# First cross attention, query stage: the key products of half 1 move behind half 0's token products of the next pair of heads

## The reference, cut to what matters

```python
q_hk = (hidden_q @ Wq.T).reshape(b, s, H, K)
q_big = jnp.einsum('bshk,hkq->bshq', q_hk, w_kc_q)
kv_rope = kv_c * cos[None] + _rotate_half(kv_c) * sin[None]
q_r = jnp.einsum('bshq,hqr->bhsr', q_big, W_qr)
k_r = jnp.einsum('bld,hdr->bhlr', kv_rope, W_kr)
scores = jnp.einsum('bhsr,bhlr->bhsl', q_r, k_r)
```

## Time and profile before

| | |
|---|---|
| median of 3 runs | 1651.32 us (1651.06 to 1651.63) |
| span of the profiled execution | 1651.2 us, 24551 instructions |
| TensorE busy | 1590.1 us, 96% |
| VectorE, ScalarE, GpSimd busy | 942.8, 731.2, 665.9 us |
| the query stage | from 354.8 to 434.5 us of the span |
| TensorE's granted clock there | 1.00 |

### The profile page before, as it was taken

The page is one execution under the profiler, slowest core; times in us unless marked ns, Lnnn a source line. Parts: engine busy times, 40 slices in busy tenths (PEclk is TensorE's granted clock), DMA queues, the critical chain, the costliest instruction groups (busy, mean ns, idle before and its releaser), DMA issues.

```text
span 1651.2 us, 24551 instructions
## 1 busy us (share of the span) xinstructions
PE 1590.1 (96%) x9832; PEld 1353.0 (82%) x9832; DVE 942.8 (57%) x1535; ACT 731.2 (44%) x1227; POOL 665.9 (40%) x483
## 2 busy tenths in 40 slices
PE   7999999989999999989999989998989999999998
PEld 7898666878899998768889976887668888888887
DVE  6555664366545455677768566354766455554554
ACT  3113655322587765666511156332635334353342
POOL 3875542441498873421137633212512422222321
PEclk9999999999999999999999999999999999999999
DMA  4110003123222007200001100110001111111111
GB/s 166 52 65 28 2 2 116 56 84 127 95 89 65 14 1 267 93 1 1 1 13 65 51 27 1 50 39 32 21 23 43 45 64 46 51 46 51 51 58 45
DMA packets 28580, 88.52 MB, mean 54 GB/s; under 512 B 4154, under 2 KB 4282, under 8 KB 28215
## 3 DMA queue, kind: packets, MB, share of 16 engines
q1 hardware_dynamic: 28468, 86.96, 15.4%
HBM read 85.11 MB, written 1.84 MB: 53 GB/s over the span
## 4 chain that ended last, share of the span: by engine, by line
PE 83%; DVE 8%; ACT 5%; issue 3%; POOL 1%; ACTq 0%; DVEq 0%; POOLq 0%
PE PS L261 19%; PE PS L263 18%; PE PS L262 18%; PE PS L266 7%; PE PS L1125 4%; PE PS L1462 3%; PE PS L1477 2%; PE PS L561 2%; PE PS L952 1%; PE PS L585 1%; PE PS L1709 1%; PE PS L1697 1%; PE PS L551 1%; DVE sm L1731 1%; PE PS L569 1%
## 5 line engine op out<-in xcount | busy, mean ns | idle before, releaser
L307 POOL TENSOR_TENSOR HL<-stg,HL 128x1024 fp32r<-128x1024 f32 (+2 forms) x111 | 243.8, 2199 | 543.5 <-ACT HL L302 525.5
L261 PE MATMUL PS<-XT,HL 128*128 128x448 f32 x608 | 225.0, 370 | 4.3 <-DVE XT L342 3.7
L263 PE MATMUL PS<-XT,HL 128*128 128x448 f32 x608 | 223.1, 367 | 0.0
L262 PE MATMUL PS<-XT,HL 128*128 128x448 f32 x608 | 223.1, 367 | 0.0
L302 ACT ACTIVATE HL<-stg 128x1024 fp32r<-128x1024 f32 (+2 forms) x111 | 104.5, 944 | 216.6 <-PE PS L263 200.9
L261 PE MATMUL PS<-HL,XT 128*128 128x512 f32 (+1 forms) x380 | 137.8, 363 | 2.2 <-DVE XT L1981 1.4
L263 PE MATMUL PS<-HL,XT 128*128 128x512 f32 (+1 forms) x380 | 134.8, 355 | 0.0
L262 PE MATMUL PS<-HL,XT 128*128 128x512 f32 (+1 forms) x380 | 134.8, 355 | 0.0
L261 PEld LDWEIGHTS PS<-XT,HL 128*128 128x128 f32 x608 | 115.0, 189 | 16.6 <-DVE XT L342 4.9
L262 PEld LDWEIGHTS PS<-XT,HL 128*128 128x128 f32 x608 | 115.1, 189 | 9.2
L263 PEld LDWEIGHTS PS<-XT,HL 128*128 128x128 f32 x608 | 114.9, 189 | 9.2
(11 more groups left out here) (299 smaller groups left out, 3813.7 us busy)
## 6 DMA issues: line engine op xcount, KB each, us to landing
stg<-in_wst SPq DMA_DIRECT2D x87, 512.0 KB, 3.2
stg<-in_wst SPq DMA_DIRECT2D x16, 352.0 KB, 3.0
stg<-in_wst SPq DMA_DIRECT2D x16, 320.0 KB, 3.2
wsum<-in_wfc SPq DMA_DIRECT2D x8, 512.0 KB, 3.7
wsum<-in_wpj SPq DMA_DIRECT2D x8, 512.0 KB, 3.5
raw<-in_wfc SPq DMA_DIRECT2D x8, 512.0 KB, 7.5
stg<-in_wst SPq DMA_DIRECT2D x16, 256.0 KB, 2.6
raw<-in_wpj SPq DMA_DIRECT2D x7, 512.0 KB, 7.0
```

Of the source, the lines that this page charges most:

```text
L261: e.matmul(out, lh, rh, start=start, stop=False)
L262: e.matmul(out, lh, rl, start=False, stop=False)
L263: return e.matmul(out, ll, rh, start=False, stop=stop)
L307: e.tensor_tensor(slot(k)[:, 1, 0:n], stg[k % NSTG][:, 0:n], slot(k)[:, 0, 0:n].bitcast(F), A.subtract).then_inc(*done("pool_w", k))
```

## The change

The key products of half 1 of pair hp are issued in the next pair, behind the token products of its half 0; those of half 0 stay behind the token products of half 1. The side products are split: token_query(hp+1) goes beside half 0, key_query(hp+2) beside half 1, both ahead of the last two token products of a half. ScalarE's and VectorE's orders follow. stream_plan and sync, with the order of the loads, stay as they are, and so do all instructions in number and size.

```diff
--- before.py
+++ after.py
@@ -923,106 +923,107 @@
             e.tensor_tensor(Krh[hp % 3][:, 1, :], stg[k % NSTG][:, 576:704], Krh[hp % 3][:, 0, :].bitcast(F),
                             A.subtract).then_inc(*done("dve_q", "K", hp))
 
+        def key_product(e, hp, half):
+            e.wait_ge(*upon("dve_q", "qr", hp, half))
+            if half == 0:
+                e.wait_ge(*upon("dve_q", "K", hp))
+            if hp:
+                e.wait_ge(*upon("dve_q", "o", hp - 1, half))
+                e.wait_ge(*upon("act_q", "o", hp - 1, half))
+            kr, qr = Krh[hp % 3], qrh[half]
+            for j, (a, c) in enumerate(((0, 0), (0, 1), (1, 0))):
+                for e_ in range(2):
+                    r0 = slice(64 * e_, 64 * e_ + 64)
+                    last = e.matmul(PS[:, kbank(half, e_, hp), 0:HT], kr[r0, a, :], qr[r0, c, :], start=j == 0, stop=j == 2)
+                    if j == 2:
+                        last.then_inc(*done("pe_q", "k", hp, half, e_))
+
         def pe_q(e):
-            def beside(st):
-                if st < 8:
-                    yield from key_query(e, st)
-                if st <= 8:
-                    yield from token_query(e, st - 1)
-
-            for st in range(2, 10):
-                side = beside(st)
-                hp, i = st - 2, st % 2
-                n_side = 6 * (st < 8) + 8 * (st <= 8)
-                n = n_done = 0
-                e.wait_ge(*upon("dve_q", "M", hp))
-                for half in range(2):
-                    if hp:
-                        e.wait_ge(*upon("dve_q", "qr", hp - 1, half))
-                    elif half:
-                        ln_turn(e, "lnx", NT - 1, xn[0], NT - 1)
-                        e.wait_ge(*upon("dve_ln", "lnx", NT - 1, "lo"))
-                    else:
-                        e.wait_ge(*upon("dve_ln", "lnx", 3, "lo"))
-                    for kc in range(4):
-                        hs = slice(half * HT, (half + 1) * HT)
-                        out = PS[:, 3 + half, 0:HT]
-                        terms = ((0, 0), (0, 1), (1, 0))
-                        for j, (a, c) in enumerate(terms):
-                            last = e.matmul(out, Mhl[i][:, a, kc, :], XT[:, c, kc, hs], start=kc == 0 and j == 0,
-                                            stop=kc == 3 and j == 2)
-                            if kc == 3 and j == 2:
-                                last.then_inc(*done("pe_q", "q", hp, half))
-                            n += 1
-                            while n_done < n_side * n // 24:
-                                next(side)
-                                n_done += 1
+            def token_product(hp, half, side, n_side):
+                n_done = 0
+                if hp:
+                    e.wait_ge(*upon("dve_q", "qr", hp - 1, half))
+                elif half:
+                    ln_turn(e, "lnx", NT - 1, xn[0], NT - 1)
+                    e.wait_ge(*upon("dve_ln", "lnx", NT - 1, "lo"))
+                else:
+                    e.wait_ge(*upon("dve_ln", "lnx", 3, "lo"))
+                hs = slice(half * HT, (half + 1) * HT)
+                for n in range(12):
+                    kc, (a, c) = n // 3, ((0, 0), (0, 1), (1, 0))[n % 3]
+                    last = e.matmul(PS[:, 3 + half, 0:HT], Mhl[hp % 2][:, a, kc, :], XT[:, c, kc, hs], start=n == 0, stop=n == 11)
+                    while n_done < n_side * (n - 1) // 8 and n_done < n_side:
+                        next(side)
+                        n_done += 1
+                last.then_inc(*done("pe_q", "q", hp, half))
                 for _ in side:
                     pass
 
-                for half in range(2):
-                    e.wait_ge(*upon("dve_q", "qr", hp, half))
-                    if half == 0:
-                        e.wait_ge(*upon("dve_q", "K", hp))
-                    if hp:
-                        e.wait_ge(*upon("dve_q", "o", hp - 1, half))
-                        e.wait_ge(*upon("act_q", "o", hp - 1, half))
-                    kr, qr = Krh[hp % 3], qrh[half]
-                    for j, (a, c) in enumerate(((0, 0), (0, 1), (1, 0))):
-                        for e_ in range(2):
-                            r0 = slice(64 * e_, 64 * e_ + 64)
-                            last = e.matmul(PS[:, kbank(half, e_, hp), 0:HT], kr[r0, a, :], qr[r0, c, :], start=j == 0, stop=j == 2)
-                            if j == 2:
-                                last.then_inc(*done("pe_q", "k", hp, half, e_))
-                    if hp == 7 and half == 0:
-                        e.wait_ge(*upon("act_q", "C", 7))
-                        x_scores(e, 0)
+            for hp in range(8):
+                e.wait_ge(*upon("dve_q", "M", hp))
+                token_product(hp, 0, token_query(e, hp + 1) if hp < 7 else iter(()), 8 * (hp < 7))
+                if hp:
+                    key_product(e, hp - 1, 1)
+                token_product(hp, 1, key_query(e, hp + 2) if hp < 6 else iter(()), 6 * (hp < 6))
+                key_product(e, hp, 0)
+            e.wait_ge(*upon("act_q", "C", 7))
+            e.wait_ge(*upon("act_q", "o", 6, 1))
+            x_scores(e, 0)
+            key_product(e, 7, 1)
 
         def act_q(e):
-            for st in range(2, 10):
-                if st < 8:
-                    key_hi(e, st)
-                    key_query_out(e, st)
-                if st == 9:
+            def parts(hp, half):
+                if hp:
+                    e.wait_ge(*upon("pe_q", "k", hp - 1, half, 1))
+                e.wait_ge(*upon("pe_q", "q", hp, half))
+                e.activation(qrh[half][:, 0, :], PS[:, 3 + half, 0:HT], ACT.Copy).then_inc(*done("act_q", "qr", hp, half))
+
+            def out(hp, half):
+                e.wait_ge(*upon("pe_q", "k", hp, half, 1))
+                e.activation(qx_at(half, 2 * hp + 1), psv(kbank(half, 1, hp)), ACT.Copy).then_inc(*done("act_q", "o", hp, half))
+
+            for hp in range(8):
+                if hp < 6:
+                    key_hi(e, hp + 2)
+                if hp < 7:
+                    token_query_hi(e, hp + 1)
+                else:
                     e.activation(expo[:, :], C("ones")[:, 0:1], ACT.Exp)
-                if st > 1:
-                    hp = st - 2
-                    for half in range(2):
-                        if hp:
-                            e.wait_ge(*upon("pe_q", "k", hp - 1, half, 1))
-                        e.wait_ge(*upon("pe_q", "q", hp, half))
-                        e.activation(qrh[half][:, 0, :], PS[:, 3 + half, 0:HT], ACT.Copy).then_inc(*done("act_q", "qr", hp, half))
-                if st <= 8:
-                    token_query_hi(e, st - 1)
-                if st > 1:
-                    hp = st - 2
-                    for half in range(2):
-                        h = 2 * hp + 1
-                        e.wait_ge(*upon("pe_q", "k", hp, half, 1))
-                        e.activation(qx_at(half, h), psv(kbank(half, 1, hp)), ACT.Copy).then_inc(*done("act_q", "o", hp, half))
+                parts(hp, 0)
+                if hp:
+                    out(hp - 1, 1)
+                if hp < 6:
+                    key_query_out(e, hp + 2)
+                parts(hp, 1)
+                out(hp, 0)
+            out(7, 1)
 
         def dve_q(e):
-            for st in range(2, 10):
-                if st < 8:
-                    key_lo(e, st)
-                if st > 1:
-                    hp = st - 2
-                    for half in range(2):
-                        e.wait_ge(*upon("act_q", "qr", hp, half))
-                        e.tensor_tensor(qrh[half][:, 1, :], PS[:, 3 + half, 0:HT], qrh[half][:, 0, :].bitcast(F),
-                                        A.subtract).then_inc(*done("dve_q", "qr", hp, half))
-                if st <= 8:
-                    token_query_lo(e, st - 1)
-                if st > 1:
-                    hp = st - 2
-                    for half in range(2):
-                        if hp == 7 and half:
-                            x_largest(e, 0)
-                        h = 2 * hp
-                        e.wait_ge(*upon("pe_q", "k", hp, half, 0))
-                        e.tensor_copy(qx_at(half, h), psv(kbank(half, 0, hp))).then_inc(*done("dve_q", "o", hp, half))
-                for b in range(NB)[st - 2 + (st > 4):st - 1 + (st > 3)]:
-                    rotate_columns(e, b)
+            def parts(hp, half):
+                e.wait_ge(*upon("act_q", "qr", hp, half))
+                e.tensor_tensor(qrh[half][:, 1, :], PS[:, 3 + half, 0:HT], qrh[half][:, 0, :].bitcast(F),
+                                A.subtract).then_inc(*done("dve_q", "qr", hp, half))
+
+            def out(hp, half):
+                e.wait_ge(*upon("pe_q", "k", hp, half, 0))
+                e.tensor_copy(qx_at(half, 2 * hp), psv(kbank(half, 0, hp))).then_inc(*done("dve_q", "o", hp, half))
+
+            for hp in range(8):
+                if hp < 6:
+                    key_lo(e, hp + 2)
```

(13 more changed lines are left out.)

## The result

The changed kernel took 1687.97 us in the median of 4 runs (1683.28 to 1691.09), the kernel before 1651.47: a ratio of 1.0219, 95% interval 1.0203 to 1.0234. It is 36.5 us slower; forecast were 12.2 us, in a range up to 1668. The profiled execution has a span of 1689.3 us and took 1691.09. In every run here the time lies about 1.8 us above the run's own span, so the median before, only 0.1 us above the profiled span, belongs to a faster execution than the profiled one. From profile to profile the difference is 38.1 us.

What follows compares the result with a forecast made beforehand. TensorE was taken as the bound, busy 1590.1 of 1651.2 us. Split key products -2.1, late qx weights +14.0 and qx7 +0.3 summed to +12.2 us, so 1663.5 us, range 1657.5 to 1668.

Steps and rivals of the forecast that it cites:

- vanished wait for the remainder: Half 1's key products would no longer wait for VectorE's remainder, a wait of 2.7 us in all over seven times.
- covers called free: kq's loads, M's parts, VectorE's rotations and the Exp table's load were said to cost nothing, hidden behind other work.
- rival D: In the query stage, TensorE's clock lowered after the stalls, adding 8 us: 1671.5 us; chance 5%.
- 12.7 forecast: Pairs 1 to 5 of the query stage would take 12.7 us each.
- The landing: The 512 KB qx load, issued 0.4 us behind a kq load, would land in 4.0 us, bounds 3.2 and 4.4.
- 14.0 forecast: Late qx weights stall token_query's first product in pairs 1 to 5, 2.8 us each: +14.0 us.
- qx7 term: In pair 5's issue, qx7 waits only for kq14's slot release and comes slightly late: +0.3 us.
- The split: Key products in two blocks save 0.31 us a pair, 0.25 in pair 0, nothing in pair 7: -2.1 us.
- price of going into and out of a key block: Each second entry and exit around a pair's key products costs 0.185 us, for seven pairs.
- B: The qx weights come in time in the query stage, so only the split counts: 1649.2 us; chance 7%.
- E: ScalarE, held by its new order, keeps the old wait, so the 2.1 us gain is missing: 1665.6 us; chance 5%.
- C: Half a stall for qx weights, 1.5 us in each of five pairs: +5.4 us, 1656.7 us; chance 5%.

Runs made afterwards that it cites:

- plan_fixed: The changed kernel with weight pieces streamed in the new order of use, qx(hp+1) ahead of kq(2hp+4) and kq(2hp+5): 1651.46 us, ratio 0.9987 to the kernel before.
- idle_long: plan_fixed, with TensorE waiting in pairs 1 to 5 for 24 small GpSimd instructions before token_query's first product: 1690.2 us, ratio 1.0235 to the kernel before.
- sides_swapped: The kernel before, unsplit, with token_query ahead of key_query among the side products and the load plan untouched: 1675.63 us, ratio 1.0133.
- qx_between: The changed kernel with qx placed between a pair's two kq loads in the plan, issued 1.5 us earlier: 1662.88 us, ratio 1.0068 to the kernel before.
- late_sides: The changed kernel with token_query's eight products behind all twelve token products of half 0: 1664.3 us, ratio 1.0069 to the kernel before.
- idle_short: plan_fixed, with TensorE waiting in pairs 1 to 5 for 10 small GpSimd instructions before token_query's first product: 1668.2 us, ratio 1.01 to the kernel before.
- sides_in_twos_b: plan_fixed with side products in twos, behind every third (half 0) or fourth (half 1) token product: 1652.21 us, ratio 1.0 to the kernel before.

## Why the prediction was wrong

**What held.** The place and the first cause of the loss did: the load of qx stands behind kq's, and TensorE waits for it in pairs 1 to 5, three token products in, with nothing in pairs 0 and 6. SyncE's issue (0.38 behind kq), the key block's 0.80 us, the vanished wait for the remainder, and covers called free were as written.

**The step that failed** is the treatment of the clock. The sum held the work behind a wait at its pace of before and put the lower clock into rival D, at 5% and 8 us. The stage shows 114.18 - 77.72 = 36.5 us more: 17.4 us of waits, 0.9 us less for the rest (77.7 to plan_fixed's 76.8), and so 20.0 us of slower work. idle_long has a like amount without any late load: 115.5 - 76.8 - 21.2 = 17.5 us. Pairs 1 to 5 took 16.6 to 19.1 us each instead of the 12.7 forecast. Without the slower work the loss would have been 16.5 us (17.4 - 0.9), at the very edge of the range.

The argument for 5% was that the stage shows a clock of 1.00 and that no wait of TensorE in the trace is longer than 2.6 us. But the trace of before has the lower clock right behind that very wait, and the prediction did not look there. First the wait and the clock behind it in the kernel before, then the same wait in plan_fixed, where the clock stayed:

```profile
705.34 0.63 PE L266 MATMUL PS<-cst,xz 128*128 128x128 f32 x4 [2.63 <-DVE XT L1327]
...
706.42:709.83 3.41, 3.41 (x10) 2.66 (x9) 2.27 (x7) 1.39 (x3) 0.94 (x2) 0.50 0.01 2
...
703.10 0.63 PE L267 MATMUL PS<-cst,xz 128*128 128x128 f32 x4 [2.63 <-DVE XT L1329]
...
700.47:713.10 12.63, 9.38 (x47) 7.40 (x47) 11.82 (x30) 5.36 (x12) 2.82 (x6) 1.00 0.00 1
```

Of the four waits of 2.0 us and more in the trace of before, two were followed by the lower clock (2.25 and 2.63 us). So five waits of near 3 us called for far more than 5%. Its price was at hand too: work at 1.2 GHz takes twice its time. In the kernel after, the five stretches at the lower level are 44.4 us, with TensorE busy for 40.4 of them; half of that is 20.2 us, and 20.0 were lost. In idle_long it is half of 35.2, or 17.6, against 17.5.

The Trainium skill's page TensorE: Matmul & The Clock Gate, in the section HAM oscillation, describes this pattern, a kernel that drops to the lower clock at each wait for a DMA and starts each tile slowly, and counts half of the time at the lower clock as lost. By that way of counting an estimate for the 44.4 us is 22.2; the trace agrees, with 20.0, once the idle part is left out.

**Terms that were mis-sized.** The landing: 4.8 to 5.6 us, taken 4.0, bound 4.4, which is 5.6 us more over the five. The weight loads' waits show it in full, 19.3 us against the 14.0 forecast. TensorE's products stood for 17.4 only. Here the prediction's sum was wrong the other way: it counted from the time at which the weight load is wanted, 0.51 us into the pair, while the third token product runs until 0.88 (366.18 to 367.06), so a wait costs the products some 0.4 us less than it said. The estimate of the landing came from loads issued in twos; here one more kq is 1.5 us ahead and the transfer has a thin tail of 1.5 us. Why these last packets are late is open: with the same three loads in sides_swapped qx landed in 4.2 to 4.8 us. In plan_fixed, where qx is issued alone, it lands in 3.1 to 3.3. The qx7 term (+0.3) was nothing. The split: -0.9 us in the stage instead of -2.1, because the side products of the new spacing cost some 0.01 us more each, 0.17 us a pair; in twos the forecast 0.31 us a pair are there and the stage is 1.9 us shorter than before. The price of going into and out of a key block, 0.185 us by rows, was right: a pair in twos takes the forecast 9.87.

**Rivals.** B (in time) and E (ScalarE holds the pair) are excluded by the waits' row and by plan_fixed. C's half wait is what qx_between and late_sides made on purpose. D was the right addition with a price too small by more than half (8 us against 20.0) and a chance far too small (5%).

## What to carry to other kernels

Whoever moves the use of a streamed operand must move its load in the same edit: with an in-order queue and few slots, a piece whose slot has long been free waits for its predecessors, and here that cost 36 us. Before a wait is called harmless, look at the granted clock right behind the waits of its length anywhere in the trace, not only in the stage that is changed. When a change puts repeated waits into a stage that runs at the full clock, price the work behind them at the lower clock too: here it cost a little more than the waits themselves (20.0 against 17.4 us).

## Not expected

- All eleven waits of TensorE over 3 us in the eleven profiles were followed by the lower clock, or had it begin within them, and so were the seven of 1.9 to 2.6 us in this stage (sides_swapped, late_sides, qx_between). Waits of 1.3 us and less in this stage were not; those of 1.5 and 1.7 us (idle_short, late_sides) were.
- Length alone does not decide it. Waits that every profile has, at the same place and of the same length, were followed in some and not in others: the 1.41 us in pair 0 once in eleven (late_sides), the 1.67 us just ahead of the stage five times, the 2.63 us of the kernel before's 705.34 five times. What decides was not tested.
- 512 KB behind two 352 KB loads took up to 5.6 us to land, against a usual 3.1 to 3.3 in plan_fixed. A single late landing needs no such neighbours: in sides_in_twos_b one qx issued alone (398.51) took 4.9 us.
- A side product costs about 0.01 us more between single token products than in the old spacing.
